# A fused convolution block with a top-two mixture of experts on one Trainium2 core: raw rows with their inverse deviation as a word, centred weights, Newton steps on VectorE, and chunks 2 and 3 routed one by one

## What is computed

```python
x = x + relu(conv3x3(layernorm_channels(x, eps=1e-6), kernel, groups=8) + bias)
t = tokens(x)                                   # 4096 x 128
z = layernorm(t, eps=1e-5)
logits = z @ router_w.T                         # 8 experts
topk_vals, topk_idx = top_k(logits, 2)
weights = softmax(topk_vals)
y_e = (silu(z @ w_gate[e]) * (z @ w_up[e])) @ w_down[e]     # 128 -> 256 -> 128
out = t + sum over the two experts of weight * y_e
```

## Time and profile before

| | before |
|---|---|
| median of 3 runs | 277.31 us (277.27 to 277.38) |
| profiled execution, its own time | 278.89 us |
| span of the profiled execution | 277.2 us |
| TensorE busy | 202.9 us (73%) |
| VectorE busy | 140.8 us (51%) |
| ScalarE busy | 119.0 us (43%) |
| GpSimd busy | 163.6 us (59%) |
| mean granted TensorE clock | 0.866 |

### The profile page before, as it was taken

One profiled execution on the slowest core, in us unless ns is written; L12 is line 12 of the kernel. 1 busy time (PEld: TensorE's weight loads), 2 busy tenths in 40 slices (PEclk: granted clock), 3 DMA queues, 4 the chain that ended last, 5 costly groups with the idle time before them and its releaser, 6 DMA issues.

```text
span 277.2 us, 4518 instructions
## 1 busy us (share of the span) xinstructions
PE 202.9 (73%) x1186; PEld 174.3 (63%) x1186; DVE 140.8 (51%) x457; ACT 119.0 (43%) x285; POOL 163.6 (59%) x184
## 2 busy tenths in 40 slices
PE   6699576975529595739998654993999999999000
PEld 5687464864428484428887544883898789898000
DVE  3557696555241724445755322451458866555025
ACT  2369544745902353073453322342445454454100
POOL 5644388743775277725777777764356576666600
PEclk9599895999957777757999999898899999999855
DMA  7993010100133351100232232343239523361075
GB/s 235 380 381 116 0 48 30 53 29 10 48 94 82 78 115 59 48 10 31 74 87 70 68 78 78 100 134 84 61 68 303 159 72 96 99 195 43 15 237 217
DMA packets 26648, 28.99 MB, mean 105 GB/s; under 512 B 4957, under 2 KB 18409, under 8 KB 26624
## 3 DMA queue, kind: packets, MB, share of 16 engines
q1 hardware_dynamic: 21776, 20.03, 25.1%
q0 software_dynamic: 4544, 8.47, 9.1%
q10 hardware_dynamic: 304, 0.20, 0.2%
HBM read 16.93 MB, written 12.67 MB: 107 GB/s over the span
## 4 chain that ended last, share of the span: by engine, by line
PE 28%; POOL 21%; issue 13%; DVE 12%; DMA 11%; SPq 6%; ACT 6%; POOLq 1%; ACTq 0%; DVEq 0%
POOL zs L992 11%; POOL yb L1005 9%; PE ps_gu L349 7%; PE ps_y L439 5%; DMA yb<-y,zt 3%; PE ps_gu L419 3%; PE ps_gu L421 3%; PE ps_gu L420 3%; PE ps_h L429 3%; SPq L303 3%; DMA zt<-zs 3%; ACT zr L547 2%; DMA spare<-yb 2%; PE ps_z L408 2%; DVE bn L637 2%
## 5 line engine op out<-in xcount | busy, mean ns | idle before, releaser
L1005 POOL DMA_INDIRECT yb<-y,zt x78 | 76.3, 978 | 40.0 <-ACT y L583 24.6
L992 POOL DMA_INDIRECT zs<-zr,slot x64 | 63.0, 984 | 38.0 <-issue 18.3
L349 PE MATMUL ps_gu<-pad,ckw 128*128 128x256 f32 x192 | 53.7, 439 | 0.0
L349 PEld LDWEIGHTS ps_gu<-pad,ckw 128*128 128x128 f32 x192 | 41.7, 224 | 7.1
L842 DVE TENSOR_TENSOR hh<-ps_gu,sg 128x512 f32<-128x512 f32 (+1 forms) x40 | 27.1, 678 | 35.7 <-ACT sg L574 35.7
L439 PE MATMUL ps_y<-wall,hT 128*128 x312 | 41.9, 278 | 0.0
L439 PEld LDWEIGHTS ps_y<-wall,hT 128*128 128x128 f32 x312 | 38.7, 195 | 0.1
L574 ACT ACTIVATE sg<-ps_gu 128x512 f32<-128x512 f32 (+1 forms) x40 | 23.5, 586 | 33.3 <-PE ps_gu L421 33.3
L583 ACT ACTIVATE y<-ps_y,zt 128x128 f32<-128x128 f32 x78 | 24.4, 365 | 30.1 <-PE ps_y L439 30.1
L419 PE MATMUL ps_gu<-wall,z_lo 128*128 x78 | 36.4, 467 | 0.0
L408 PE MATMUL ps_z<-ident,zt 128*128 128x128 f32 x78 | 17.1, 302 | 21.2 <-DMA zt<-zs 15.2
(11 more groups left out here) (131 smaller groups left out, 225.9 us busy)
## 6 DMA issues: line engine op xcount, KB each, us to landing
zt<-zs SPq DMA_DIRECT2D x78, 65.0 KB, 2.0
spare<-yb SPq DMA_DIRECT2D x16, 256.0 KB, 4.5
xt<-x_rows SPq DMA_DIRECT2D x8, 256.0 KB, 5.3
xc<-x_cols SPq DMA_DIRECT2D x8, 256.0 KB, 6.6
spare<-gate_up_w SPq DMA_DIRECT2D x8, 256.0 KB, 6.3
out<-xt SPq DMA_DIRECT2D x8, 256.0 KB, 3.0
yb<-y,zt POOLq DMA_INDIRECT x78, 2.3
zs<-nulls SPq DMA_DIRECT2D x18, 65.0 KB, 3.3
```

The costliest lines, as they stand in the source:

```text
L349: last = nc.tensor.matmul(dst, ckw[:, h * BANDS + k, :], pad[n % 2][:, h * IMG:(h + 1) * IMG, below:below + PAIRS, dx:dx + WW], start=k == ...
L992: nc.gpsimd.indirect_dma_start(zs[g], bass.IndirectOffsetOnAxis(slot[:, k, n * TT + t:n * TT + t + 1], 0), zr[n % ZR][:, t, k, :], None, b ...
L1005: nc.gpsimd.indirect_dma_start(yb, bass.IndirectOffsetOnAxis(zt[:, u % RING, s, P:P + 1].bitcast(U32), 0), y[u % YB][:, s, :], None, bound ...
```

## The change

- Rows are no longer normalised before they are sent. `rows` holds each row of a chunk twice, as it is, with three words behind it: the row number, the token's weight and the row's inverse deviation (`ROW` is 131 words, before 130). `normalise_t`, `write_ids`, `write_weights` and the four buffers `zr` are gone; ScalarE copies the rows twice and writes the words (`row_scalars`).
- The mean is taken out of the weights in place of the rows: TensorE multiplies each expert's gate and up weights with a centring matrix (`centre_weights`) into one PSUM bank `ps_w`; ScalarE takes the head from it and VectorE the tail, and only then may the next expert's product be made. The router is centred in the same way. GpSimd makes no tails any more.
- In the experts the inverse deviation is applied as a per-row scale, by silu on ScalarE and by the product on VectorE, each now one instruction for each tile in place of one for two.
- The inverse deviations of the rows (except batch 0) and of the inputs of chunks 4 to 7 come from VectorE: a start value and three Newton steps, ten dependent instructions (`inverse_root`), in place of one power on GpSimd.
- Chunks 2 and 3 are two batches in place of one. Counts are passed from batch to batch through the rank matmuls (`pass_on`).
- The last batch is routed ahead of phase 2; the pad copies of chunks 2 to 7 are ScalarE's alone; `ps_t` is one buffer in place of two; logits come before the transposes; input loads are reordered; and `table(1)` moves from unit 3 and 10 to units 0 and 1.

The core of the diff:

```diff
-BATCHES = [(0, 1), (1, 2), (2, 4), (4, 6), (6, 8)]
-SETS = [(0, 3), (3, 5)]
+BATCHES = [(0, 1), (1, 2), (2, 3), (3, 4), (4, 6), (6, 8)]
+SETS = [(0, 4), (4, 6)]
...
+ID, WEIGHT, RSTD = P, P + 1, P + 2
...
-        xt = sb("xt", [P, CHUNKS * TT, P])
+
+        rows = sb("rows", [P, 2, CHUNKS * TT, ROW])
+        xt = rows[:, 0, :, 0:P]
...
+                for t in range(TT):
+                    last = nc.tensor.transpose(ps_t[:, t * P:(t + 1) * P], xc[:, n, t * P:(t + 1) * P], ident[:])
+                last.then_inc(t_rows_ready, 1)
+
...
+            def centre_weights(e):
+                pe.wait_ge(ew_loaded[e], 16)
+                if e >= 1:
+                    pe.wait_ge(w_lo_ready, e)
+                nc.tensor.matmul(ps_w, centre[:], ew[:, e], start=True, stop=True).then_inc(w_ready_ps, 1)
...
+                e = 2 * (n - CENTRE_STEP)
+                if 0 <= e < E:
+                    centre_weights(e)
                 conv(n, 1)
-                for b, (c0, c1) in enumerate(BATCHES):
-                    if n == c1:
-                        rank(b)
+                if n - 1 in BATCH_AT:
+                    rank(BATCH_AT[n - 1])
+                if 0 <= e < E:
+                    centre_weights(e + 1)
                 if n == SET_CHUNKS[0][1] + 1:
...
+                for k in range(2):
+                    nc.scalar.copy(rows[:, k, n * TT:(n + 1) * TT, 0:P], ps_t.rearrange("p (t c) -> p t c", t=TT)
+                                   ).then_inc(t_copied, 1)
...
+            def row_scalars(b):
+
+                i, c = tiles_of(BATCHES[b]), (BATCHES[b][1] - BATCHES[b][0]) * TT
                 act.wait_ge(gap_ready, b + 1)
+                nc.scalar.copy(rows[:, :, i, RSTD], rstd2[:, i].rearrange("p (o t) -> p o t", o=1)
+                               .broadcast_to([P, 2, c]))
                 if b >= 1:
                     act.wait_ge(w_ready, b)
                 nc.scalar.activation(th[:], gap_n[:], ACT.Tanh, scale=0.5).then_inc(th_ready, 1)
+                act.wait_ge(th_ready, b + 1)
+                nc.scalar.activation(rows[:, 0, i, WEIGHT], th[:, 0:c], ACT.Identity, bias=half[:, 0:1],
+                                     scale=half[:, 0:1])
+                nc.scalar.activation(rows[:, 1, i, WEIGHT], th[:, 0:c], ACT.Identity, bias=half[:, 0:1],
+                                     scale=half[:, 1:2]).then_inc(w_ready, 1)
...
-                act.wait_ge(ew_loaded[e], 16)
-                nc.scalar.copy(wall3[:, e, 0:2 * H], ew[:, e]).then_inc(w_hi_ready, 1)
+                act.wait_ge(w_ready_ps, e + 1)
+                nc.scalar.copy(wall3[:, e, 0:2 * H], ps_w).then_inc(w_hi_ready, 1)
...
+                for s in range(COUNT[u]):
+                    last = nc.scalar.activation(sg[u % 2][:, s, :], ps_gu[u % 2][:, s * N:s * N + H], ACT.Silu,
+                                                scale=zt[:, u % RING, s, RSTD:RSTD + 1])
+                last.then_inc(sg_ready, 1)
...
             for n in range(CHUNKS + 1):
+                e = 2 * (n - CENTRE_STEP)
                 if n >= 1:
                     conv_relu(n - 1, 1)
-                if 1 <= n and n + 1 < CHUNKS:
+                if 0 <= e - 2 < E:
+                    weight_heads(e - 1)
+                if n - 2 in BATCH_AT:
+                    row_scalars(BATCH_AT[n - 2])
+                if 1 <= n < CHUNKS - 1:
                     normalise_x(n + 1)
                 if n < CHUNKS:
                     conv_relu(n, 0)
-                if n + 1 < CHUNKS:
-                    pad_evens(n + 1)
                 if n >= 1:
...
-                        normalise_t(c0 + 1)
+                if n + 1 < CHUNKS:
...
+            def inverse_root(v, dst):
+
+                c = v.shape[-1]
+                s = newtons[0]
+                newtons[0] += NEWTON_STEPS
+                r, r_next = guess[0][:, 0:c], guess[1][:, 0:c]
+                nc.vector.tensor_scalar(r.bitcast(I32), v.bitcast(I32), -0.5, MAGIC, ALU.mult, ALU.add
+                                        ).then_inc(newton_step, 1)
+                for k in range(3):
+                    to = dst if k == 2 else r_next
+                    dve.wait_ge(newton_step, s + 3 * k + 1)
+                    nc.vector.scalar_tensor_tensor(square[:, 0:c], r, -0.5, r, ALU.mult, ALU.mult
+                                                   ).then_inc(newton_step, 1)
+                    dve.wait_ge(newton_step, s + 3 * k + 2)
+                    nc.vector.tensor_tensor(scaled[:, 0:c], square[:, 0:c], v, ALU.mult).then_inc(newton_step, 1)
+                    dve.wait_ge(newton_step, s + 3 * k + 3)
+                    nc.vector.scalar_tensor_tensor(to, scaled[:, 0:c], 1.5, r, ALU.add, ALU.mult
+                                                   ).then_inc(newton_step, 1)
+                    r, r_next = r_next, r
+                dve.wait_ge(newton_step, s + NEWTON_STEPS)
...
-                dve.wait_ge(rstd1_made, group + 1)
+                i = tiles_of(X_GROUPS[group])
...
+                else:
+                    dve.wait_ge(ve1_ready, group + 1)
+                    inverse_root(ve1[:, i], rstd1[:, i])
...
+                if b >= POOL_BATCHES:
+                    dve.wait_ge(ve2_ready, b + 1)
+                    inverse_root(ve2[:, i], rstd2[:, i])
...
+                for s in range(COUNT[u]):
+                    last = nc.vector.scalar_tensor_tensor(
+                        hh[u % 2][:, s, :], ps_gu[u % 2][:, s * N + H:(s + 1) * N], zt[:, u % RING, s, RSTD:RSTD + 1],
+                        sg[u % 2][:, s, :], ALU.mult, ALU.mult)
+                last.then_inc(h_ready, 1)
...
+            dve.wait_ge(iod_ready, 6 + len(SETS))
             for n in range(CHUNKS):
-                for b, (c0, c1) in enumerate(BATCHES):
-                    if n == c1 + 1:
-                        slots(b)
-                        write_weights(b)
-                if n >= 1:
-                    residual(n - 1)
+                e = 2 * (n - CENTRE_STEP)
+                if 0 <= e < E:
+                    weight_tails(e)
+                residual(n)
+                if n - 1 in BATCH_AT:
+                    slots(BATCH_AT[n - 1])
+                    if not closes(BATCH_AT[n - 1]):
+                        pass_on(BATCH_AT[n - 1])
+                if n in (2, 4):
...
+                stats_t(n)
+                if n == SET_CHUNKS[0][1]:
                     table(0)
...
+                if n in BATCH_AT:
+                    deviation_t(BATCH_AT[n])
+                if 0 <= e < E:
+                    weight_tails(e + 1)
+                if n in BATCH_AT:
+                    top_two(BATCH_AT[n])
+                    scale_gap(BATCH_AT[n])
+            slots(LAST)
...
+            alone = CHUNKS - 2
+            for n in range(alone):
+                dispatch(n, 0, 2 * TT)
```

466 lines of the change are left out of this document (183 added, 283 removed).

## The result

| | before | after |
|---|---|---|
| median | 277.35 us (277.27 to 278.94, 4 runs) | 294.74 us (291.39 to 295.98, 4 runs) |
| profiled execution, its own time | 278.89 us | 295.76 us |
| span | 277.2 us | 293.9 us |
| TensorE, VectorE, ScalarE, GpSimd busy | 202.9, 140.8, 119.0, 163.6 us | 213.6, 154.0, 124.8, 151.7 us |

The change makes the kernel slower: the ratio is 1.057, 95% interval 1.046 to 1.068. Forecast were 293.7 us for the median and 295.3 for an execution like the profiled one.

What follows compares the result with a forecast made beforehand. Phase 1 was taken as bound by hand-overs, paced by VectorE's masks. Stretches up to GpSimd's first combine summed to +16.4 us, giving 295.3 us for a profiled execution and 293.7 for the median, range 280 to 300.

Steps and rivals of the forecast that it cites:

- To the first rank, -3.2: Start of phase 1: two input statistics and weight-head casts no longer precede chunk 0's rows; 31.2 becomes 28.0 us.
- Chunk 1, -0.5: Stretch to chunk 1's rank: convolution, logits, statistics, Newton steps and mask sum to 12.6 us against 13.1.
- restart: TensorE's convolution after a wait over 3 us: 2.5 us more for the low clock; 1.5 at the first rank.
- Chunks 2 and 3, +15.5: Phase 1, now two batches: shift delays normalisation, tails delay products; 16.5 and 19.1, together 35.6 us against 20.1.
- Chunks 4 and 5, +7.3: Phase 1: shift, normalisation, tails and products make 37.2 us against 29.9, though the 7.8 us buffer wait goes.
- Chunks 6 and 7, -4.4: End of phase 1: 18.1 us against 22.5, where the last mask stood behind unit 0 in VectorE's list.
- To the first combine, +1.7: After the last rank: units 0 to 2 run at low clock with a table between; 13.9 us against 12.2.
- The signs: Expected in the trace: mask waits for chunks 1 to 3, TensorE's longest at products, last rank near 131, combine near 145.
- A (the clock holds): Rival on TensorE in phase 1: restarts after waits lose nothing, so +4.9, 282.2 us; chance 0.20.
- B (the waits are covered): Rival in phase 1: tails 1 and 3 and the shifts are ready in time; -2.4, 274.9 us; chance 0.11.
- C: Rival on GpSimd: its queue sets the end anyway, earlier feeding and later masks cancel, no change; chance 0.03.
- D: Rival: the unit loop loses its slack and more pieces run at low clock; +23, 300 us; chance 0.05.

Runs made afterwards that it cites:

- together: The changed kernel with chunks 2 and 3 routed together again as one batch: 291.18 us, ratio 1.048 to before.
- tails first: The changed kernel with each expert's weight tail moved ahead of the statistics in VectorE's list, same instructions: 286.8 us, ratio 1.034 to before.
- statistics first: The changed kernel with the statistics of x for chunks 4 to 7 one step earlier in VectorE's list: 288.14 us, ratio 1.038 to before.
- one Newton iteration: The changed kernel with one Newton iteration in place of three, 4 small steps in place of 10: 287.16 us, ratio 1.035 to before.
- all three: The changed kernel with chunks 2 and 3 together, tails behind the slots and statistics of x a step earlier: 277.72 us, ratio 1.0003 to before.
- before, split: The kernel before with only chunks 2 and 3 routed one by one: 279.27 us, ratio 1.001 beside a before of 277.5 us.
- the fourth comparison: Last set of runs, undisturbed: before with the split (279.27 us) and the changed kernel with three orders changed (277.72 us), beside before at 277.5 us.
- one disturbed comparison: Dummy matmuls added in TensorE's waits of the changed kernel: 313.53 us against the changed kernel's 320.4 us, beside a before of 312.6 us.
- the single edits: Four kernels, each the changed kernel with one edit (chunks 2 and 3 together, tails, statistics or Newton steps): 286.8 to 291.18 us.

## Why the prediction was right

The forecast went by stretches between ranks. By the same marks (us; first rank, then the length of each stretch to the next one, and from the last rank to the first combine):

| | first rank | chunk 1 | 2 and 3 | 4 and 5 | 6 and 7 | to combine | first to last combine |
|---|---|---|---|---|---|---|---|
| before | 31.17 | 13.10 | 20.09 | 29.97 | 22.47 | 12.18 | 132.37 |
| forecast | 28.0 | 12.6 | 35.6 | 37.2 | 18.1 | 13.9 | as before |
| after | 28.27 | 12.95 | 34.07 | 36.50 | 18.47 | 13.97 | 132.41 |
| together | 26.63 | 11.20 | 29.87 | 37.28 | 18.48 | 13.96 | 135.04 |
| tails first | 26.52 | 12.96 | 30.99 | 29.21 | 21.59 | 13.99 | 134.49 |
| statistics first | 26.67 | 13.16 | 31.14 | 31.86 | 18.48 | 13.97 | 133.75 |
| one Newton iteration | 26.39 | 11.81 | 30.05 | 34.08 | 17.25 | 15.60 | 133.08 |
| all three | 26.79 | 13.14 | 23.74 | 25.46 | 22.93 | 14.00 | 134.99 |
| before, split | 30.48 | 13.07 | 27.27 | 24.33 | 20.98 | 13.24 | 131.54 |

- **To the first rank, -3.2**: measured -2.9, in part by luck. In eight of the nine later traces whose lists are the same up to there the first rank comes at 26.4 to 26.8, which would be -4.4 to -4.8.
- **Chunk 1, -0.5**: -0.15. It holds one restart that other executions were spared (11.2 us and not 13.0, see the last section).
- **Chunks 2 and 3, +15.5**: +14.0. Chunk 2 alone hit, 16.45 for 16.5, and its mechanism (the shift ahead of the normalisation) is shown by the kernel with statistics first, where it falls to 12.6. Chunk 3 took 17.62 for 19.1. The mis-sized term is the restart, 6.0 for each of its two pairs of product and convolution: the first (58.68 to 63.89) took 5.21, with 4.25 for the convolution, and the second, from 70.33 to the rank at 75.29, 4.96. There the product took 1.84 and not 0.85, and the convolution 3.1 and not 5.15.
- **Chunks 4 and 5, +7.3**: +6.5. The same pair ahead of their rank took 5.99 (105.80 to 111.79), as forecast, but by luck: the product took 1.84 for 0.85 and the convolution 4.15 for 5.15. The pair at 90.18 took 5.27 for 6.0. The waits of 4.6 at the products, and their hanging on a tail behind statistics and Newton steps, are shown by the kernel with tails first (-7.3 in this stretch).
- **Chunks 6 and 7, -4.4**: -4.0. **To the first combine, +1.7**: +1.8.
- **A Newton step of 0.20**: 0.197. The centring product (0.88) takes 0.86 to 0.94 to the start of the next matmul where the clock is full, and 1.84 behind a wait of 4.6, for which the forecast had no term. The silu pair took 0.84 and not 0.95, the product pair on VectorE 0.88; units late in phase 2 still follow each other in 2.94 us, so nothing was lost there, as forecast.
- The sum: the first combine at 144.23 for 145.4. The 1.2 us too much in phase 1 were made up by 1.4 behind the last combine, a term I had at nothing (in the other traces of the changed lists it is 15.9 to 17.2 us long, so it scatters). So the profiled execution (295.76 for 295.3) is nearer than its parts deserve.
- **The signs**: last rank, first combine, the dispatches of chunk 4 (115.61), ScalarE's waits for the shift and TensorE's for a tail came as written. Two did not. The rank of chunk 3 has no mask wait, as the sum itself had it (6.0 for TensorE against 3.3 for the mask), and TensorE's longest wait is 7.32 for the last mask, not at a product.
- **Restarts by the length of the wait**: the forecast charged 2.5 behind waits over 3 us. The traces don't sort them so. The convolution behind the first rank took 4.52 or 2.84 us after the same wait of 1.86, and the one behind chunk 1's rank 4.38 after 3.95 here, but 2.84 in one Newton iteration's kernel after 2.80.
- **The noise**: 0.2% was too good. Before alone ran from 275.05 to 280.21 in the fourth comparison, and the intervals of the ratios reach 0.4 to 1.1% to each side.

Of the rivals, A (the clock holds) described a part of the kernel that really can be won back, and overstated its price: 11.5 forecast, 4.0 to 6.9 in one disturbed comparison. B (the waits are covered) gave 274.9 and decided at tail 3; the kernel with all three orders is near that case, made by hand and without the split, with 277.72. C is refuted by the loss itself and by the single edits: the first combine comes 6.8 to 9.1 us earlier in them, and the median falls by 3.6 to 7.9. D did not occur.

## What to carry to other kernels

Where engines run lists in order, cost a new step by what stands behind it, not by its length: four tails of 0.69 us cost 6.5 to 8 us through their place, and moving them gave it back with no instruction saved. When a change brings a hand-over between three engines (product, head, tail), put each link ahead of long work that nobody waits for. Judge a split of a batch in the kernel where it will live: in the kernel before, its price of 7.2 us was paid back, 5.6 of it by a buffer freed earlier; in the changed one, which had no such wait, 4.2 us of price brought 0.8 back.
